# Attention and a binarised feed-forward on one core: the absolute values of the weight differences, one attention step later

## What is computed

```python
x = x + attention(layernorm(x), ...)           # softmax(q k^T / 4) v, per head

def _binary_diff_weight(w, base):
    d = w - base
    coeff = jnp.mean(jnp.abs(d))
    return base + coeff * jnp.sign(d)

W1, W2, W3 = [_binary_diff_weight(w, m) for w, m in ((w1, mean_w1), (w2, mean_w2), (w3, mean_w3))]
h = jax.nn.silu(y @ W1.T) * (y @ W3.T)
x = x + h @ W2.T
```

## Time and profile before

| | |
|---|---|
| median of three runs | 990.76 us |
| the profiled execution | 986.26 us, its span 984.5 us |
| granted TensorE clock, mean | 0.989 |
| attention steps, first to last exponential | 52.8 to about 461 us |
| signs L1086, 42 of them | starts 90.0 to 420.2 us, median 632 ns |
| absolute values L1088, 42 of them | starts 99.6 to 430.7 us, median 652 ns and 222 ns |

### The profile page before, as it was taken

How to read it: one execution, slowest core, us unless ns; L and a number is a source line. 1 busy time by engine, 2 the same in 40 slices (tenths; PEclk the granted TensorE clock), 3 DMA queues, 4 the chain that set the end, 5 groups by cost and what they waited for, 6 DMA issues and landing times.

```text
span 984.5 us, 14763 instructions
## 1 busy us (share of the span) xinstructions
PE 945.6 (96%) x5030; PEld 619.7 (63%) x5030; DVE 712.2 (72%) x948; ACT 547.2 (56%) x1076; POOL 303.7 (31%) x312
## 2 busy tenths in 40 slices
PE   7899999999999999988899999999999999999997
PEld 6534433443344433333688888888888888888886
DVE  6778898789888898867965588555885558854443
ACT  5468889889998998966544323233232332332220
POOL 5864567466646422445000101111010110101110
PEclk9979999999999999999999999999999999999999
DMA  5535655565545566624642002400023100220001
GB/s 181 139 111 172 193 165 170 148 192 171 167 129 179 180 187 209 192 82 136 212 140 75 1 1 86 143 34 1 1 86 136 39 0 0 85 86 0 0 0 43
DMA packets 75668, 105.14 MB, mean 107 GB/s; under 512 B 9944, under 2 KB 33496, under 8 KB 75608
## 3 DMA queue, kind: packets, MB, share of 16 engines
q1 hardware_dynamic: 74776, 103.26, 33.2%
q0 software_dynamic: 448, 0.46, 0.3%
q10 hardware_dynamic: 384, 0.66, 0.2%
HBM read 74.59 MB, written 28.05 MB: 104 GB/s over the span
## 4 chain that ended last, share of the span: by engine, by line
PE 80%; DVE 6%; ACT 4%; issue 3%; POOL 3%; SPq 2%; DMA 1%; ACTq 0%; DVEq 0%; POOLq 0%
PE psum L1750 15%; PE psum L1751 15%; PE psum L1752 15%; PE psum L1649 9%; PE psum L1639 8%; PE psum L1623 6%; PE psum L1530 3%; PE psum L1531 2%; ACT probs L1075 2%; DVE nmx L1260 1%; PE psum L1662 1%; PE psum L1663 1%; PE psum L1739 1%; DVE stage L1375 1%; PE psum L1519 1%
## 5 line engine op out<-in xcount | busy, mean ns | idle before, releaser
L1260 DVE TENSOR_REDUCE nmx<-psum 128x2 f32<-128x1024 f32 x256 | 304.9, 1220 | 57.3 <-PE psum L1623 55.2
L1075 ACT ACTIVATE probs<-psum 128x512 f32<-128x512 f32 x512 | 270.9, 603 | 42.6 <-PE psum L1639 40.9
L932 POOL CAST dh<-w2T 128x512 fp32r<-128x512 f32 (+1 forms) x56 | 49.3, 880 | 419.2 <-PE psum L1752 403.7
L1750 PE MATMUL psum<-fxh,wh 128*128 128x512 f32 x448 | 175.4, 392 | 0.0
L1751 PE MATMUL psum<-fxl,wh 128*128 128x512 f32 x448 | 174.5, 390 | 0.0
L1752 PE MATMUL psum<-fxh,wl 128*128 128x512 f32 x448 | 174.4, 389 | 0.0
L1639 PE MATMUL psum<-q_slot,k_slot 50*128 50x512 f32 x512 | 150.4, 472 | 14.2 <-ACT probs L1075 7.8
L1639 PEld LDWEIGHTS psum<-q_slot,k_slot 50*128 50x128 f32 x512 | 64.3, 186 | 130.6 <-ACT probs L1075 64.0
L1649 PE MATMUL psum<-probs,v_slot 128*32 128x512 f32 x1024 | 138.4, 613 | 0.0
L1131 ACT ACTIVATE hh<-gate 128x512 fp32r<-128x512 f32 x56 | 35.4, 632 | 171.6 <-DVE gate L1444 171.6
L1444 DVE TENSOR_TENSOR gate<-gate,psum 128x512 f32<-128x512 f32 x56 | 38.3, 685 | 124.7 <-PE psum L1752 123.0
(11 more groups left out here) (146 smaller groups left out, 1330.5 us busy)
## 6 DMA issues: line engine op xcount, KB each, us to landing
stage<-in_L_ffn_mean_w_dram SPq DMA_DIRECT2D x60, 256.0 KB, 3.7
q_slot<-q_stack SPq DMA_DIRECT2D x180, 64.0 KB, 2.3
stage<-in_L_ffn_w_dram SPq DMA_DIRECT2D x42, 256.0 KB, 3.7
weighted_values<-u_sb SPq DMA_DIRECT2D x32, 256.0 KB, 2.4
k_slot<-k_stack SPq DMA_DIRECT2D x60, 96.0 KB, 2.4
an<-weighted_values SPq DMA_DIRECT2D x16, 256.0 KB
al<-reciprocals SPq DMA_DIRECT2D x16, 256.0 KB
x<-_attn_hidden_states_dram SPq DMA_DIRECT2D x8, 512.0 KB, 4.4
```

The source lines that it names most:

```text
L932: nc.gpsimd.tensor_copy(dh[parity][:], w2T[:, bass.ds(src, 1), :].rearrange("p o c -> p (o c)")).then_inc(dh_ok, 1)
L1075: nc.scalar.activation(probs[kt][:, j, :], BANK[ring_bank(("score", g, kt, j))], ACT.Exp, scale=HEAD_DIM ** -0.5).then_inc(exp_ok, 1)
L1260: v.tensor_reduce(column, pair, AX.X, ALU.max, negate=True).then_inc(s_max, 1)
L1750: mm(o, lhs_hi, rhs_hi, start=first, stop=False)
```

## The change

All three absolute values of a tile move one step down ScalarE's queue: from kt = 1, 2, 3 of the odd group to kt = 2, 3 of the odd group and kt = 0 of the next even group. Steps with kt = 2 and 3 hold one as before (of another matrix). The steps kt = 1 of the odd groups lose theirs; the steps kt = 0 of the even groups (16, 24, ..., 120) gain one, behind `copy_u`. The instructions are the same.

```diff
-SIGN_LAG = 2
+SIGN_LAG, ABS_LAG = 2, 4
...
                 if 0 <= k < 3:
                     act.wait_ge(fd_ok, 3 * e + k + 1)
                     nc.scalar.activation(sgn[:, e, k, :], wn[e % 3][:, k, :], ACT.Sign).then_inc(fsgn_ok, 1)
-                if 3 <= k < 6:
-                    nc.scalar.activation(wn[e % 3][:, k - 3, :], wn[e % 3][:, k - 3, :], ACT.Abs,
-                                         accum_out=dsum[:, k - 3, e:e + 1]).then_inc(facc_ok, 1)
+                k -= ABS_LAG
+                if 0 <= k < 3:
+                    nc.scalar.activation(wn[e % 3][:, k, :], wn[e % 3][:, k, :], ACT.Abs,
+                                         accum_out=dsum[:, k, e:e + 1]).then_inc(facc_ok, 1)
```

## The result

| | before | changed |
|---|---|---|
| median, us | 990.9 (20 runs) | 997.18 (20 runs) |
| lowest to highest | 986.48 to 999.01 | 994.61 to 1002.57 |
| ratio to before, 95% interval | | 1.0069 (1.0053 to 1.0084), so 5.3 to 8.3 us |
| profiled execution, its span | 986.26, 984.5 | 997.76, 996.0 |
| first score tile of the last step | 458.4 | 468.9 |

The forecast was 995.9, with a range of 991.0 to 999.5. The two profiled executions differ by 11.5 us, more than the medians do (6.3): that of before is near the low end of its runs, that of the changed kernel is not. Which part of the 11.5 is the change's is therefore read step by step.

What follows compares the result with a forecast made beforehand. It took TensorE to bound the kernel, with no slack behind `copy_u`; delays of 1.86 + 1.24 + 1.70 + 0.62 = 5.42, less 0.27, gave 5.15 us on the 990.76 median: 995.9 us, range 991.0 to 999.5.

Steps and rivals of the forecast that it cites:

- The old place: kt = 1 of odd groups: the absolute value fits ScalarE's 0.75 us of idle time, so removal is worth 0 each.
- The new place: Behind `copy_u` at kt = 0 of even groups: no slack, each absolute value delays the next exponential by 0.62 us.
- A projection beside: Steps 17, 41, 49, 73, 81, with half a projection beside: 0.28 of 0.62 is slack, 1.70 us in all.
- Steps 25, 57 and 89: Steps following the new place, near waits on other engines or loads: 0.31 us each for 25 and 57, 0 for 89.
- step 109: Exception among the removals, where ScalarE is the chain: a gain of 0.27 us, between 0 and 0.61.
- Step 121: Follows the last new place; ScalarE idles 2.60 us before its first exponential, so a cost of 0.
- The sum: All terms of the attention steps together: 5.42 less 0.27, so 5.15 us more.
- the span up to the feed-forward: Sign to look for in the changed trace: this span about 5 us longer, the feed-forward itself equal.
- Rival B: No change: ScalarE has room and other waits take up the step delays; 990.8, up to 1 us more; chance 0.09.
- Rival C: Faster: all 14 removed absolute values are paid for now, new ones covered behind `copy_u`; 8.7 us less, 982.1; chance 0.03.
- Rival D: Slower by over 1%: 0.89 us each in 13 steps, 1002.4, or a second late shift DMA; chance 0.06.

Runs made afterwards that it cites:

- experiment 1: The kernel before, with the absolute value at kt = 1, the first of each tile, cut to one column; median 990.6 us, ratio 0.9986 (0.9959 to 1.0013).
- the control: The changed kernel's code with `ABS_LAG = 3`, restoring the instruction order of before; median 992.34 us, ratio 0.9996 (0.9968 to 1.0024) to the kernel before.

## Why the prediction was right, point by point

- **The old place is free: right.** 0.76 of idle time stands where the absolute value was, step 101 lasts 3.42 with it, without it, and with one column of it.
- **The new place is exposed, 0.62 each: right.** 0.61 from the absolute value to the exponential in step 97, 0.62 with the new place added, and 0.60 to 0.61 in each of the five steps that were taken at the full price. The Trainium skill, "ScalarE: Activation LUTs", "What ACT_TABLE_LOAD costs", gives, as an estimate from its 186 ns, 0.833 ns per element and 93 ns of overlap, 0.52 for 512 elements; the trace agrees up to the accumulator row (365.21 to 365.73) and has 0.09 more behind it.
- **A projection beside hides 0.28: right.** It was worked out from a sign in step 13, and all five steps grew by 0.34 or 0.35.
- **Steps 25, 57 and 89: each wrong, their sum nearly right by luck.** The prediction took 0.31, 0.31 and 0. Step 25 gave back 0.60 of its 0.61 two steps later, at VectorE's maxima and not at GpSimd's subtraction, which the prediction had named; 57 gave back nothing; 89 cost 0.42, of which 0.21 came back in steps 94 and 95. The load of the keys gave back nothing: step 93, in which it lands, keeps its 3.42. Together 0.01 + 0.58 + 0.21 = 0.80, where 0.62 was taken. A half as a guess for "between nothing and all" was the value of none of them.
- **0.27 back at step 109: right**, 0.25 in step 110, and 0.25 again with the old place emptied.
- **Step 121: 0, as far as can be seen.** It took 3.21 before and 4.38 in the changed profile, but it takes 4.38 with the old place emptied too, where nothing stands ahead of it, at the same clock of 0.50.
- **The sum: 5.15 forecast, 5.3 by the steps.** The medians say 6.3, the interval 5.3 to 8.3. What is over the steps, about 1 us, isn't assigned. That the late transfer comes later or oftener with the new place isn't excluded by one profile of each kernel; those taken show no sign of it.
- **A sign that failed: the span up to the feed-forward.** It should have been about 5 us longer, the feed-forward equal. Up to the start of the last step it was 10.5 longer, and 1.1 behind it. This compares two single executions, and the steps at a low clock are in it; the prediction didn't foresee them.
- **Rival B** rested on TensorE's share and ScalarE's room. The Trainium skill, "Perfetto Trace Analysis", "Identifying the Most-Contended Engine", would have the engine with the highest occupancy optimised first. TensorE's busy share (95%) names the right engine here, though the Trainium skill would judge TensorE there by its FLOPs and its weight loads (62%, below VectorE's 71%); neither share says what this change costs: ScalarE was busy for 55%, and 14 of its instructions, moved by one step, made TensorE wait for 5 us. Rival C falls by experiment 1. Rival D's price of 0.89 falls by the 0.61 of step 97; its other door, a late transfer, opened in the profile, but it opens with the order of before as well.

## What to carry to other kernels

A place in an engine's queue has a price that its busy share doesn't tell. Look at what ended the idle time before the next instruction that the bound engine waits for: if that is the bound engine itself, an instruction fits in for nothing up to the idle time; if there is none, each instruction is paid one to one. To check a term of some tenths of a us in a kernel that scatters by 10 us, count it in step lengths; the row of waits for that one producer tells the orders apart (here 63.4 to 64.0 in the three kernels with nothing added behind `copy_u`, 69.5 and 71.0 with the absolute value there), the difference of two spans doesn't.

## What the runs showed that was not expected

- **The late small transfer.** 8 KB took 5.26 to 7.98 us to land in step 103 in the twelve profiles, with the DMA engines at a share of 0.93 at the end of that step in the changed kernel; the step lasted 3.71 to 6.66, where steps without such a wait last 2.60.
- **The clock after a wait.** A stretch in which TensorE was busy for 0.44 of 4.04 us was followed by a step at a granted clock of 0.50 that took 4.06 for 2.60. In the changed kernel the step after it, 105, had 0.74 and took the 3.50 that the absolute value gives it anyway. In the control it stayed at 0.50 and took 4.38 for 2.90: there a step 103 that was 0.9 us longer than before (4.90 against 4.04) was followed by two steps that took 2.9 us more.
- **The same in step 121.** TensorE's waits for VectorE's `oy` are the same in both profiles (6.1 us in three), yet steps 121 and 122 had a clock of 0.84 and 0.77 in the profile of before, and 0.50 and 0.61 in the changed one, and took 8.55 and 10.82. The changed order isn't needed for it: the two take 10.94 with the old place emptied and 10.04 in the control. What makes one execution fall and another not stays open.
